# The batch loop of an attention and expert kernel is written out, and its down product changes sides

## The chip, the cores and the metric

The kernel runs on one core of one Trainium2 chip. The metric is the device time of one execution in microseconds (us), as the median of several runs. Five engines matter here: TensorE (PE in the rows, with its weight loads as PEld), VectorE (DVE), ScalarE (ACT), GpSimd (POOL) and SyncE (SP), which issues the transfers. Each works through its own list of instructions in order, and they wait for each other through semaphores.

## The reference

For a batch of 8 sequences of 1024 tokens with 256 channels, all in float32:

```python
# first half
qkv = x @ Wqkv + bqkv                       # q, k, v: 1024 x 256 each
q2, k2 = normalised squares of centred q, k
kv = einsum('bnc,bnd->bcd', k2, v)
t2 = einsum('bnc,bcd->bnd', q2, kv) / sqrt(N)
x1 = layernorm(x + (v + t2) @ Wln + bln)
# second half: 16 experts of width 128
sel    = sigmoid(einsum('bsd,ed->bse', x1, expert_sel))
scores = relu(einsum('bsd,edh->bseh', x1, keys))
out    = einsum('bseh,ehv,bse->bsv', scores, values, sel)
result = layernorm(x1 + out)
```

## The kernel before, in words

Every float32 operand of a product is split into a high part (`_h`) and a low part (`_l`), and `product` (line 990) makes three matmuls of it: high by high, high by low, low by high. Each matmul has its own weight load.

The second half sets the frame. A batch is 32 steps: two groups (`g`) of 512 tokens, 16 experts (`e`) each. In step `s` TensorE makes the up product of expert `e` into `up_bank[s % 2]`: hidden units by tokens, 6 matmuls of 512 columns. VectorE turns it into `gated` (relu times the spread gate `sel_all`, line 962), ScalarE copies the high part `gated_h` (line 509), VectorE subtracts to get `gated_l` (line 972). One step later (`LAG = 1`) TensorE adds the down product into two PSUM banks, `down_bank[0]` and `down_bank[1]`, which collect a group's 16 experts. GpSimd spreads the next gate row (line 495).

The first half of the next batch is laid between these products by a hand-written table, `LOOP["plan"]`: at each step it names the stages that TensorE runs between up and down product. QK projects queries and keys, GG adds to the k-by-x matrix, KS and KV finish it, QT transposes q, Y makes the layer's output, XT transposes `x1`, LG makes the gate logits. The stages in `RING_KINDS` share two PSUM banks, `ring_bank`, in turn; a stage waits until the stage two places before it has been read.

A group ends in step 16 (or in step 0 of the next batch). Before the change its down banks hold channels by tokens. ScalarE copies both to `oT` (the end of its `step`, lines 661 to 675; line 509 in the profile), the stage OT transposes them back with 4 transposes for each pair of token tiles (line 1108), and VectorE adds `x1` into `z` (line 923), followed by the statistics (lines 928, 931) and the scaling. The first down product of the next group waits for `o_copied`, since it overwrites the banks.

All engines run the same function `run`: the start (`it = -1`), batch 0, then a hardware loop over batches 1 to 6, then batch 7 and a short end (`it = 8`, table `LAST`). GpSimd has a loop of its own over the groups.

Of the kernel before, what the change touches and what calls it, by code (L numbers as in the profile page):

```python
# [26 lines left out]
ALU = mybir.AluOpType  # L27
# [60 lines left out]
RING_KINDS = ("QT", "Y", "XT", "LG", "OT", "KS", "KV")  # L88
# [30 lines left out]
def stages(it, s):  # L119

    out = []
    for kind, a in schedule(it)["plan"].get(s, ()):
        if kind == "OT":
# [18 lines left out]
def build_program(nc, x, xT, wqk, wvT, wln, b_qk, b_v, b_ln, esel, keys, values, ident_in, out):  # L142
    with ExitStack() as ctx:
# [6 lines left out]
        def sem(name):  # L150
# [48 lines left out]
        oT = sb("oT", [P, M, GN])  # L199
# [5 lines left out]
        w_stage = [oT[:].rearrange("p a n -> p (a n)"), z[:].rearrange("p a t c -> p (a t c)")]  # L205
# [55 lines left out]
        o_copied = sem("o_copied")  # L261
        (o_transposed, z_added, z_stated, z_aggregated, z_rooted, z_inverted, z_shift_made, out_made) = map(sem, (
            "o_transposed", "z_added", "z_stated", "z_aggregated", "z_rooted", "z_inverted",
# [29 lines left out]
        def ring_place(it, s, kind, a):  # L293

            rep = it if isinstance(it, int) else 1
            n = RING_AT[(rep, s, kind, a)]
            if n < 2:
                return ring_bank[n % 2], None, 0
            pit, ps, pkind, pa, poff = RING[n - 2]
            b = it + (pit - rep) + poff  # L300
            if pkind == "OT":
                return ring_bank[n % 2], z_added, out_pair(it + (pit - rep), poff, pa)
# [20 lines left out]
        def run(eng, step):  # L323

            for s in range(FIRST_STEP, STEPS):
                step(-1, s)
            for s in range(STEPS):
                step(0, s)
            with eng.Fori(1, B - 1) as it:
                for s in range(STEPS):  # L330
                    step(it, s)
            for s in range(STEPS):
                step(B - 1, s)
            for s in range(LAST_STEPS):
                step(B, s)
# [51 lines left out]
        def _(sp):  # L387
# [48 lines left out]
            def step(it, s):  # L436
                if isinstance(it, int) and (it, s) in PIECE_LOADS:
                    i = 2 + PIECE_LOADS.index((it, s))

                    sp.wait_ge(piece_lo, i - 1)  # L440
                    load_piece(i)
                if s == 0 and has(it, 1):
                    load_half(it, 0)
                if s == 7 and has(it, 1) and not (isinstance(it, int) and it < 0):
                    load_half(it, 1)
                for kind, a, off in planned(it, s, ("LG", "OT")):
# [11 lines left out]
        def _(pool):  # L458
# [43 lines left out]
            with pool.Fori(1, B * G) as grp:  # L502
                spread_group(grp)
# [3 lines left out]
        def _(act):  # L507
# [80 lines left out]
            def late(it, s):  # L588
                for kind, a, off in planned(it, s - 1, ("OT",)):
# [5 lines left out]
                for kind, a, off in transposed_first(  # L595
                        planned(it, s, ("QK", "GG", "KV", "QT", "Y", "XT", "LG", "OT"))):
# [39 lines left out]
                    elif kind == "OT":  # L636
                        n = out_pair(it, off, a)
                        act.wait_ge(z_aggregated, 2 * n)
                        nc.scalar.activation(z_std[:, a], z_mv[:, a, :, 1], ACT.Sqrt,
                                             bias=eps_ln[:]).then_inc(z_rooted, 1)  # L640

            def step(it, s):
# [18 lines left out]
                if (s - LAG) % E == E - 1 and step_exists(it, s, LAG):  # L661
                    f = step_no(it, s, LAG)
                    grp = 2 * it + ((s - LAG) // E)
                    if last_iteration(it):
                        act.wait_ge(last_half_made, 1)
                    else:
                        act.wait_ge(down_made, f + 1)

                    at_least(act, o_transposed, 2 * grp)
                    if first_group(it, (s - LAG) // E):  # L670

                        act.wait_ge(piece_lo, WPIECES)
# [11 lines left out]
        def _(dve):  # L684
# [108 lines left out]
            def early(it, s):  # L793
                for kind, a, off in transposed_first(
                        planned(it, s - 1, ("QK", "GG", "KS", "KV", "QT", "Y", "XT", "OT"))):
# [47 lines left out]
                    elif kind == "OT":  # L843
# [8 lines left out]
                        if last_iteration(it):  # L852
                            layer_norm(z[:, a, 1], z[:, a, 1], z_mv[:, a, 1],
                                       z_rstd[:, a, 1:2]).then_inc(last_out_made, 1)

            def late(it, s):
# [33 lines left out]
                for kind, a, off in planned(it, s, ("KS", "KV", "Y", "LG", "OT")):  # L890
# [23 lines left out]
                    elif kind == "OT":  # L914
                        n = out_pair(it, off, a)
                        t = GT * (off % G) + 2 * a
                        dve.wait_ge(o_transposed, n)

                        at_least(dve, stored[a], it * (16 * G) + off * 16)
                        if isinstance(it, int) and it == 0:  # L920

                            dve.wait_ge(piece_lo, WPIECES)
                        V.tensor_tensor(z[:, a].rearrange("p t c -> p (t c)"), ring_of(it, s, kind, a)[:],
                                        x1[:, t:t + 2].rearrange("p t c -> p (t c)"),
                                        ALU.add).then_inc(z_added, 1)
# [17 lines left out]
            def step(it, s):  # L943
# [21 lines left out]
                if last_iteration(it) and s == LAG - 1:  # L965
                    dve.wait_ge(down_made, B * STEPS)
                    at_least(dve, o_transposed, 2 * (G * B - 1))
                    V.tensor_copy(oT[:, 1], down_bank[1][:]).then_inc(o_copied, 1)
# [12 lines left out]
        def _(pe):  # L981
# [35 lines left out]
            def layer1(it, s):  # L1017
                for kind, a, off in planned(it, s, ("QK", "GG", "KS", "KV", "QT", "Y", "XT", "LG", "OT")):
# [82 lines left out]
                    elif kind == "OT":  # L1101
                        n = out_pair(it, off, a)
                        pe.wait_ge(o_copied, n - a - 1 + M)
                        for i in range(2):
                            for m in range(M):
                                j = (i * M + m) * P
                                t = 2 * a + i
                                last = nc.tensor.transpose(bk[:, j:j + P], oT[:, m, t * P:(t + 1) * P], ident[:])  # L1108
                        last.then_inc(o_transposed, 1)

            def step(it, s):
# [16 lines left out]
                if step_exists(it, s, LAG):  # L1128
# [61 lines left out]
```

## Time and profile before

| | before |
|---|---|
| median of 3 runs | 1080.75 us (1080.56 to 1083.31) |
| the profiled execution | 1078.57 us |
| its span, first to last instruction | 1076.7 us |
| PE busy | 1026.5 us, 95% |
| DVE busy | 802.1 us, 74% |
| ACT busy | 525.6 us, 49% |
| mean granted clock of TensorE | 0.987 of full speed |

The span is what the rows below divide up; the time of the execution has 1.87 us around it. Busy time of an engine is the union of its instructions, so TensorE, whose matmuls overlap each other in the pipeline, is read by the distance from one start to the next and not by the duration of one. A granted clock of 1.00 is 2.4 GHz, 0.50 is 1.2 GHz.

### The profile page before, as it was taken

What the parts mean: (1) busy time and instruction counts of PE and PEld (TensorE: products, weight loads), DVE (VectorE), ACT (ScalarE), POOL (GpSimd) and SP (SyncE); (2) the same over time, 40 slices, a digit from 0 to 9 for tenths busy, and PEclk for the clock granted to TensorE, in tenths of its full rate; (3) what the DMA queues carried; (4) which work ended last, traced back from release to release, by engine and by line L of the source; (5) the groups of instructions that cost most, each with busy time, mean ns of one, the idle gap of its engine ahead of it and who ended that gap; (6) DMA issues with size and microseconds to landing.
All of it is one profiled execution on the core that took longest, in us unless ns stands there. A gap on an engine that the chain in (4) does not pass through costs nothing.

```text
span 1076.7 us, 17466 instructions
## 1 busy us (share of the span) xinstructions
PE 1026.5 (95%) x5228; PEld 863.6 (80%) x5228; DVE 802.1 (74%) x1819; ACT 525.6 (49%) x1223; POOL 216.1 (20%) x273
## 2 busy tenths in 40 slices
PE   5789999999989999899998999989999899999996
PEld 4668888888868888688887888878888788888885
DVE  6888887878757877578775878668787678867564
ACT  5555643475334653356533565245653456434332
POOL 2121222212221121121122121221122112221221
PEclk9999999999999999899999999999999999999999
DMA  5031000100011000110001100011000110000000
GB/s 174 24 116 60 3 20 33 68 1 2 22 41 59 1 1 19 41 59 2 10 10 41 58 2 20 0 41 58 2 20 0 60 39 1 20 1 21 1 20 20
DMA packets 12089, 32.01 MB, mean 30 GB/s; under 512 B 1792, under 2 KB 2048, under 8 KB 12032
## 3 DMA queue, kind: packets, MB, share of 16 engines
q1 hardware_dynamic: 12032, 31.42, 8.4%
q14 instruction: 41, 0.34, 0.1%
q8 instruction: 16, 0.26, 0.1%
HBM read 22.50 MB, written 8.39 MB: 29 GB/s over the span
## 4 chain that ended last, share of the span: by engine, by line
PE 90%; DVE 4%; issue 3%; ACT 2%; DMA 0%; ACTq 0%; DVEq 0%
PE down_bank L990 32%; PE up_bank L990 32%; PE ring_bank L990 9%; PE qk_bank L990 8%; PE g_bank L990 4%; PE ring_bank L1108 1%; PE ring_bank L1089 1%; PE ring_bank L1073 1%; DVE gated L962 1%; PE ring_bank L1099 1%; PE ring_bank L1098 1%; PE ring_bank L1054 1%; ACT oT L509 0%; ACT gated_h L509 0%; DMA x<-in_wqk 0%
## 5 line engine op out<-in xcount | busy, mean ns | idle before, releaser
L509 ACT ACTIVATE gated_h<-gated 128x512 fp32r<-128x512 f32 x256 | 161.3, 630 | 397.3 <-DVE gated L962 397.3
L495 POOL PARTITION_BROADCAST sel_all<-sel_rows x240 | 193.0, 804 | 744.8 <-DVE gated L962 744.0
L962 DVE SCALAR_TENSOR_TENSOR gated<-up_bank,sel_all 128x512 f32<-128x512 f32 x256 | 176.0, 687 | 85.3 <-PE up_bank L990 69.3
L990 PE MATMUL down_bank<-gated_h,vals_h 128*128 128x512 f32 x512 | 210.2, 411 | 19.2 <-ACT oT L509 18.4
L972 DVE TENSOR_TENSOR gated_l<-gated,gated_h 128x512 fp32r<-128x512 f32 x256 | 179.0, 699 | 45.3 <-ACT gated_h L509 45.3
L990 PE MATMUL up_bank<-x1T_h,keys_h 128*128 128x512 f32 x512 | 202.8, 396 | 0.0
L990 PE MATMUL up_bank<-x1T_h,keys_l 128*128 128x512 f32 x512 | 202.6, 396 | 0.0
L990 PE MATMUL down_bank<-gated_h,vals_l 128*128 128x512 f32 x512 | 202.2, 395 | 0.0
L990 PE MATMUL down_bank<-gated_l,vals_h 128*128 128x512 f32 x512 | 201.6, 394 | 0.0
L990 PE MATMUL up_bank<-x1T_l,keys_h 128*128 128x512 f32 x512 | 200.7, 392 | 0.0
L990 PEld LDWEIGHTS down_bank<-gated_h,vals_h 128*128 128x128 f32 x512 | 96.9, 189 | 39.0 <-ACT oT L509 19.6
L990 PEld LDWEIGHTS up_bank<-x1T_h,keys_l 128*128 128x128 f32 x512 | 97.0, 189 | 22.2
L990 PEld LDWEIGHTS down_bank<-gated_h,vals_l 128*128 128x128 f32 x512 | 96.8, 189 | 22.4
L990 PEld LDWEIGHTS up_bank<-x1T_l,keys_h 128*128 128x128 f32 x512 | 97.1, 190 | 21.7
L990 PEld LDWEIGHTS up_bank<-x1T_h,keys_h 128*128 128x128 f32 x512 | 97.2, 190 | 20.3
L990 PEld LDWEIGHTS down_bank<-gated_l,vals_h 128*128 128x128 f32 x512 | 97.2, 190 | 15.2
L758 DVE TENSOR_TENSOR qk<-qk_bank,qk_bias 128x512 f32<-128x512 f32 x60 | 41.3, 688 | 36.2 <-PE qk_bank L990 36.2
L990 PE MATMUL qk_bank<-wqk_h,xT_h 128*128 128x512 f32 x120 | 49.7, 414 | 9.6 <-DVE xT_l L738 9.6
L990 PE MATMUL qk_bank<-wqk_h,xT_l 128*128 128x512 f32 x120 | 48.3, 402 | 0.0
L990 PE MATMUL qk_bank<-wqk_l,xT_h 128*128 128x512 f32 x120 | 48.2, 402 | 0.0
L771 DVE TENSOR_TENSOR y<-ring_bank,x_raw 128x256 f32<-128x256 f32 x64 | 27.0, 422 | 27.5 <-PE ring_bank L990 26.9
L509 ACT ACTIVATE k_h<-k,k_scale 128x256 fp32r<-128x256 f32 x64 | 32.6, 509 | 28.9 <-DVE k_scale L805 28.2
(160 smaller groups left out, 1710.2 us busy)
## 6 DMA issues: line engine op xcount, KB each, us to landing
xT_raw<-in_xT SPq DMA_DIRECT2D x16, 512.0 KB, 3.7
x_raw<-in_x SPq DMA_DIRECT2D x16, 512.0 KB, 4.6
out<-z SPq DMA_DIRECT2D x32, 256.0 KB, 2.5
oT<-in_keys SPq DMA_DIRECT2D x4, 512.0 KB, 4.2
z<-in_values SPq DMA_DIRECT2D x4, 512.0 KB, 4.4
sel_rows<-sel SPq DMA_DIRECT2D x64, 8.0 KB
x<-in_wqk SPq DMA_DIRECT2D x1, 512.0 KB, 3.4
sel_all<-in_b_qk SPq DMA_DIRECT2D x1, 256.0 KB, 6.1
```

The source lines that it names most:

```text
L495: nc.gpsimd.partition_broadcast(sel_all[:, e % 2], row, P).then_inc(sel_spread, 1)
L509: return nc.scalar.activation(dst, src, ACT.Copy, **kw)
L758: V.tensor_tensor(qk_of(it, t)[:], qk_bank_of(it, t)[:], qk_bias[:], ALU.add).then_inc(qk_biased, 1)
L771: V.tensor_tensor(y[:, a % 2], ring_of(it, s, "Y", a)[:, 0:C], x_raw[:, a], ALU.add).then_inc(y_added, 1)
L962: V.scalar_tensor_tensor(out=gated[:], in0=up_bank[s % 2][:], scalar=0.0, in1=sel_all[:, s % 2], op0=ALU.max, op1=ALU.mult).then_inc(gate_ ...
L972: V.tensor_tensor(gated_l[:, s % 2], gated[:], gated_h[:, s % 2].bitcast(F32), ALU.subtract).then_inc(gated_lo, 1)
L990: last = mm(dst, lhs, rhs, start=start and i == 0, stop=stop and i == n - 1, **kw)
L1054: last = mm(bk[:, j:j + 2], total[:, m * P:(m + 1) * P], ones[:, 0:2], start=True, stop=True)
L1073: last = nc.tensor.transpose(bk[:, j:j + P], q2[:, 2 * a + i, m * P:(m + 1) * P], ident[:])
L1089: last = nc.tensor.transpose(bk[:, m * P:(m + 1) * P], x1[:, a, m * P:(m + 1) * P], ident[:])
L1098: mm(bk[:], esel_hl[:, m], x1T_h[:, a, m], start=(m == 0), stop=False)
L1099: last = mm(bk[:], esel_h[:, m], x1T_l[:, a, m], start=False, stop=(m == M - 1))
```

## The change

Three things change. The hardware loops of all engines become Python loops, so that each engine's list of instructions holds all batches one after the other, with constants in its waits. The down product takes the gated tokens as weights and the values as the moving side, so that its banks hold tokens by channels: `down_bank[a]` has token tiles 2a and 2a+1, 256 columns each. And the stage OT goes: no copies to `oT`, no transposes; VectorE adds `x1` to a down bank directly (stage ZA, new function `add_zs`), and what followed the addition keeps its place as stage ZN. The staging buffer of the weights, which shared the room of `oT`, gets its own, `w_room`, of the same size.

```diff
 LOOP plan
-        0: [("QT", 2)], 1: [("QT", 3)], 2: [("OT", 0), ("Y", 4)], 3: [("OT", 1)], 4: [("Y", 5)],
+        0: [("QT", 2)], 1: [("ZA", 0), ("ZA", 1), ("QT", 3)], 2: [("ZN", 0), ("Y", 4)], 3: [("ZN", 1)], 4: [("Y", 5)],
...
-        16: [("GG", 5)], 17: [("QK", 7)], 18: [("GG", 6)], 19: [("KS", 0), ("OT", 0), ("GG", 7)],
-        20: [("OT", 1)], 21: [("KV", 0), ("QT", 0)], 22: [("QT", 1)], 23: [("Y", 0)],
+        16: [("GG", 5)], 17: [("ZA", 0), ("ZA", 1), ("QK", 7)], 18: [("GG", 6)], 19: [("KS", 0), ("ZN", 0), ("GG", 7)],
+        20: [("ZN", 1)], 21: [("KV", 0), ("QT", 0)], 22: [("QT", 1)], 23: [("Y", 0)],
...
-LAST = dict(plan={1: [("OT", 0), ("OT", 1)]}, split_xT={}, split_x={}, bias_x={}, scale_q={},
+LAST = dict(plan={1: [("ZA", 0), ("ZA", 1), ("ZN", 0), ("ZN", 1)]}, split_xT={}, split_x={}, bias_x={}, scale_q={},
...
 run
-            with eng.Fori(1, B - 1) as it:
+            for it in range(1, B):
                 for s in range(STEPS):
                     step(it, s)
-            for s in range(STEPS):
-                step(B - 1, s)
...
 gpsimd
-            with pool.Fori(1, B * G) as grp:
+            for grp in range(1, B * G):
                 spread_group(grp)
...
 scalar, at the end of step
-                    for m in range(M if not last_iteration(it) else 1):
-                        copy(oT[:, m], down_bank[m][:]).then_inc(o_copied, 1)
...
 vector
+            def add_zs(it, s):
+                for kind, a, off in planned(it, s, ("ZA",)):
+                    n = out_pair(it, off, a)
+                    t = GT * (off % G) + 2 * a
+                    if last_iteration(it) and a == 0:
+                        dve.wait_ge(last_half_made, 1)
+                    else:
+                        dve.wait_ge(down_made, it * STEPS + (off + 1) * E)
+
+                    at_least(dve, stored[a], it * (16 * G) + off * 16)
+                    if isinstance(it, int) and it == 0:
+
+                        dve.wait_ge(piece_lo, WPIECES)
+                    V.tensor_tensor(z[:, a].rearrange("p t c -> p (t c)"), down_bank[a][:],
+                                    x1[:, t:t + 2].rearrange("p t c -> p (t c)"),
+                                    ALU.add).then_inc(z_added, 1)
...
 vector, step
+                add_zs(it, s)
                 if step_exists(it, s):
                     f = step_no(it, s)
                     dve.wait_ge(up_made, f + 1)
...
 tensor, step
-                    if e == 0:
-
-                        at_least(pe, o_copied, M * grp)
-                    for c in range(M):
-                        r = (s - LAG) % 2
-                        if c == 1 and last_iteration(it):
+                    r = (s - LAG) % 2
+                    for t in range(GT):
+                        a, i = divmod(t, 2)
+                        if e == 0 and i == 0:
+
+                            at_least(pe, z_added, 2 * grp - 1 + a)
+                        if t == 2 and last_iteration(it):
                             last.then_inc(last_half_made, 1)
-                        last = product(down_bank[c][:], [(both(vals_h, vals_l, ALL, e, slice(c * P, (c + 1) * P)),
-                                                          both(gated_h, gated_l, ALL, r, ALL))],
-                                       start=(e == 0), stop=(e == E - 1))
+
+                        last = product(down_bank[a][:, i * C:(i + 1) * C],
+                                       [(both(gated_h, gated_l, ALL, r, slice(t * P, (t + 1) * P)),
+                                         both(vals_h, vals_l, ALL, e, ALL))],
+                                       start=(e == 0 and i == 0), stop=(e == E - 1),
+                                       skip_group_check=True)
                     last.then_inc(down_made, 1)
```

On TensorE, this is the first down product of a group before the change, in step 1 of the loop body, behind the transposes of QT 3:

```order
L1073 MATMUL ring_bank0<-ident,q2 128x128 x4
L1132 REGISTER_ALU
L285 REGISTER_ALU
L990 MATMUL down_bank0<-gated_h,vals_h 128x512
L990 MATMUL down_bank0<-gated_l,vals_h 128x512
L990 MATMUL down_bank0<-gated_h,vals_l 128x512
L990 MATMUL down_bank1<-gated_h,vals_h 128x512
L990 MATMUL down_bank1<-gated_l,vals_h 128x512
L990 MATMUL down_bank1<-gated_h,vals_l 128x512
```

And a down product now:

```order
L974 MATMUL down_bank0<-vals_h,gated_h 128x256
L974 MATMUL down_bank0<-vals_l,gated_h 128x256
L974 MATMUL down_bank0<-vals_h,gated_l 128x256
L974 MATMUL down_bank0<-vals_h,gated_h 128x256
L974 MATMUL down_bank0<-vals_l,gated_h 128x256
L974 MATMUL down_bank0<-vals_h,gated_l 128x256
L974 MATMUL down_bank1<-vals_h,gated_h 128x256
L974 MATMUL down_bank1<-vals_l,gated_h 128x256
L974 MATMUL down_bank1<-vals_h,gated_l 128x256
L974 MATMUL down_bank1<-vals_h,gated_h 128x256
L974 MATMUL down_bank1<-vals_l,gated_h 128x256
L974 MATMUL down_bank1<-vals_h,gated_l 128x256
```

Six matmuls of 512 columns have become twelve of 256, each with a weight load; the register instructions, which the loop's waits needed, are gone.

On VectorE, steps 0 to 2 of the loop body before (`gated` and `gated_l` are the two passes of each step, `z` is the addition of `x1`):

```order
L962 SCALAR_TENSOR_TENSOR gated<-up_bank0,sel_all 128x512
L972 TENSOR_TENSOR gated_l<-gated,gated_h 128x512
L831 ISA
L832 TENSOR_TENSOR qT_l<-ring_bank1,qT_h 128x512
L958 REGISTER_ALU
L962 SCALAR_TENSOR_TENSOR gated<-up_bank1,sel_all 128x512
L972 TENSOR_TENSOR gated_l<-gated,gated_h 128x512
L831 REGISTER_ALU
L832 TENSOR_TENSOR qT_l<-ring_bank0,qT_h 128x512
L958 REGISTER_ALU
L962 SCALAR_TENSOR_TENSOR gated<-up_bank0,sel_all 128x512
```

The addition of the first pair came behind this last row, in step 2, from `ring_bank1`. The same steps now, up to step 1:

```order
L950 SCALAR_TENSOR_TENSOR gated<-up_bank0,sel_all 128x512
L956 TENSOR_TENSOR gated_l<-gated,gated_h 128x512
L812 TENSOR_TENSOR qT_l<-ring_bank1,qT_h 128x512
L849 TENSOR_TENSOR z<-down_bank0,x1 128x512
L849 TENSOR_TENSOR z<-down_bank1,x1 128x512
L950 SCALAR_TENSOR_TENSOR gated<-up_bank1,sel_all 128x512
```

Both additions now stand one behind the other in step 1, ahead of that step's `gated`.

The end of VectorE's loop body before; the list of the changed kernel has no such branch on any engine but the one at its start and the one at its end:

```order
L962 SCALAR_TENSOR_TENSOR gated<-up_bank1,sel_all 128x512
L935 TENSOR_SCALAR q2<-q2,q_scale 128x256 x2
L972 TENSOR_TENSOR gated_l<-gated,gated_h 128x512
L329 REGISTER_ALU
L329 COMPARE_AND_BRANCH
```

The jump back, taken five times on each engine that runs `run`, is gone.

## Rows read from the trace of the kernel before

**Rows 1.** The page, busy time, share of the span, instructions.

```profile
PE 1026.5 (95%) x5228; PEld 863.6 (80%) x5228; DVE 802.1 (74%) x1819; ACT 525.6 (49%) x1223; POOL 216.1 (20%) x273
```

**Rows 2.** The waits: who waited for whom, total us, times, longest.

```profile
PE down_bank L990 <- ACT oT L509: 18.4, 5, 3.7
```

**Rows 3.** Windows: batch 1, then batches 2 to 6; PEclk is the granted clock.

```profile
189.00:314.80 125.80, 125.80 (x653) 106.57 (x652) 97.49 (x224) 63.64 (x150) 25.13 (x32) 1.00 0.07 25
314.80:969.30 654.50, 636.10 (x3261) 537.20 (x3260) 492.01 (x1127) 322.81 (x757) 129.30 (x161) 0.99 0.07 24
```

**Rows 4.** Timeline (start, duration, what, idle before) where batch 2 begins.

```profile
317.37 0.69 DVE L962 SCALAR_TENSOR_TENSOR gated<-up_bank,sel_all 128x512 f32<-128x512 f32 x1 [4.64 <-PE up_bank L990]
...
319.31 1.08 ACT L509 ACTIVATE oT<-down_bank 128x512 f32<-128x512 f32 x2
...
320.45 0.51 PE L990 MATMUL down_bank<-gated_h,vals_h 128*128 128x512 f32 x1 [3.64 <-ACT oT L509]
```

**Rows 5.** Windows: just behind that wait.

```profile
321.20:324.60 3.40, 3.40 (x9) 2.63 (x9) 1.49 (x2) 0.70 (x2) 0.73 (x1) 0.50 0.00 0
```

**Rows 6.** The chain that ended last, batch 2: start, us, what.

```profile
401.17 0.44 PE ring_bank L1108 x4
401.61 1.39 PE down_bank L990 x6
...
404.38 1.38 PE ring_bank L990 x12
...
412.17 1.42 PE ring_bank L990 x12
...
432.54 1.37 PE down_bank L990 x6
```

**Rows 7.** The same chain in batch 0: a GG stage, and KS.

```profile
97.49 0.70 PE g_bank L990 x6
...
139.31 0.79 PE ring_bank L1054 x8
```

**Rows 8.** Timeline of PE: first and last of 48 matmuls of stage Y.

```profile
46.84 0.36 PE L990 MATMUL ring_bank<-wvl_h,xT_h 128*128 128x256 f32 x1 [0.26 <-DVE kvw_l L827]
...
52.49 0.28 PE L990 MATMUL ring_bank<-kvw_h,qT_l 128*128 128x256 f32 x1
```

**Rows 9.** Groups of instructions by line: busy us, mean ns, idle before.

```profile
L1108 PE MATMUL ring_bank<-ident,oT 128*128 128x128 f32 x128 | 19.6, 277 | 0.9 <-DVE oT L968 0.9
```

**Rows 10.** Timeline of DVE and PE, steps 1 to 3 of batch 1.

```profile
189.52 0.68 DVE L832 TENSOR_TENSOR qT_l<-ring_bank,qT_h 128x512 fp32r<-128x512 f32 x1
190.61 0.69 DVE L962 SCALAR_TENSOR_TENSOR gated<-up_bank,sel_all 128x512 f32<-128x512 f32 x1 [0.41 <-PE up_bank L990]
190.76 0.48 PE L990 MATMUL down_bank<-gated_h,vals_h 128*128 128x512 f32 x1
...
197.46 0.66 DVE L972 TENSOR_TENSOR gated_l<-gated,gated_h 128x512 fp32r<-128x512 f32 x1
198.57 0.48 PE L990 MATMUL down_bank<-gated_h,vals_h 128*128 128x512 f32 x1
```

**Rows 11.** Timeline of DVE and PE, step 17 of batch 1.

```profile
256.86 0.68 DVE L744 TENSOR_TENSOR x_l<-x_raw,x_h 128x512 fp32r<-128x512 f32 x1
257.54 0.69 DVE L962 SCALAR_TENSOR_TENSOR gated<-up_bank,sel_all 128x512 f32<-128x512 f32 x1
258.75 0.39 PE L990 MATMUL down_bank<-gated_h,vals_h 128*128 128x512 f32 x1
```

**Rows 12.** Timeline of DVE at the end of the kernel.

```profile
1067.24 0.69 DVE L968 COPY oT<-down_bank 128x512 f32<-128x512 f32 x1 [1.74 <-PE down_bank L990]
...
1069.47 0.75 DVE L928 BATCH_NORM_STATS2 z_stats<-z 128x6 f32<-128x256 f32 x2
...
1070.36 0.67 DVE L923 TENSOR_TENSOR z<-ring_bank,x 128x512 f32<-128x512 f32 x1
...
1071.06 0.75 DVE L928 BATCH_NORM_STATS2 z_stats<-z 128x6 f32<-128x256 f32 x2
```

More of the change, by code:

```diff
@@ L83 @@
     gpsimd_xT=(1,), gpsimd_x=())
[L85 removed]
+LAST = dict(plan={1: [("ZA", 0), ("ZA", 1), ("ZN", 0), ("ZN", 1)]}, split_xT={}, split_x={}, bias_x={}, scale_q={},
             gpsimd_xT=(), gpsimd_x=())
 LAST_STEPS = 3
[L88 removed]
+RING_KINDS = ("QT", "Y", "XT", "LG", "KS", "KV")
 FIRST_STEP = min(FIRST["split_xT"])
@@ L122, in stages @@
     for kind, a in schedule(it)["plan"].get(s, ()):
-        if kind == "OT":
+        if kind in ("ZA", "ZN"):
             g = 0 if s >= E else -1
@@ L198, in build_program @@
         gated_h, gated_l = sb("gated_h", [P, 2, GN], F32R), sb("gated_l", [P, 2, GN], F32R)
-        oT = sb("oT", [P, M, GN])
+        w_room = sb("w_room", [P, WPIECE])
         z = sb("z", [P, 2, 2, C])
@@ L202, in build_program @@
         z_std, z_rstd, z_shift = (sb(n, [P, 2, 2]) for n in ("z_std", "z_rstd", "z_shift"))
-        w_stage = [oT[:].rearrange("p a n -> p (a n)"), z[:].rearrange("p a t c -> p (a t c)")]
+        w_stage = [w_room[:], z[:].rearrange("p a t c -> p (a t c)")]
         wqk_raw = x1[:, 0:4, :].rearrange("p (m a) c -> p m a c", m=M)
@@ L260, in build_program @@
         last_half_made = sem("last_half_made")
-        o_copied = sem("o_copied")
-        (o_transposed, z_added, z_stated, z_aggregated, z_rooted, z_inverted, z_shift_made, out_made) = map(sem, (
-            "o_transposed", "z_added", "z_stated", "z_aggregated", "z_rooted", "z_inverted",
+        (z_added, z_stated, z_aggregated, z_rooted, z_inverted, z_shift_made, out_made) = map(sem, (
+            "z_added", "z_stated", "z_aggregated", "z_rooted", "z_inverted",
             "z_shift_made", "out_made"))
@@ L445, in step @@
                     load_half(it, 1)
-                for kind, a, off in planned(it, s, ("LG", "OT")):
+                for kind, a, off in planned(it, s, ("LG", "ZN")):
                     if kind == "LG":
@@ L588, in late @@
             def late(it, s):
-                for kind, a, off in planned(it, s - 1, ("OT",)):
+                for kind, a, off in planned(it, s - 1, ("ZN",)):
                     n = out_pair(it, off, a)
@@ L595, in late @@
                 for kind, a, off in transposed_first(
-                        planned(it, s, ("QK", "GG", "KV", "QT", "Y", "XT", "LG", "OT"))):
+                        planned(it, s, ("QK", "GG", "KV", "QT", "Y", "XT", "LG", "ZN"))):
                     b = it + off
@@ L635, in late @@
                         copy(sel[:], ring_of(it, s, kind, a)[LOW:LOW + E, :]).then_inc(logits_low, 1)
-                    elif kind == "OT":
+                    elif kind == "ZN":
                         n = out_pair(it, off, a)
@@ L660, in step @@
                     weights_hi(PIECE_STEPS.index((it, s)))
[L661 to L672, printed above, removed]
-                    for m in range(M if not last_iteration(it) else 1):
-                        copy(oT[:, m], down_bank[m][:]).then_inc(o_copied, 1)
             act.wait_ge(constants_set, 4)
@@ L794, in early @@
                 for kind, a, off in transposed_first(
-                        planned(it, s - 1, ("QK", "GG", "KS", "KV", "QT", "Y", "XT", "OT"))):
+                        planned(it, s - 1, ("QK", "GG", "KS", "KV", "QT", "Y", "XT", "ZN"))):
                     b = it + off
@@ L842, in early @@
                                         ALU.subtract).then_inc(x1T_lo, 1)
-                    elif kind == "OT":
+                    elif kind == "ZN":
                         n = out_pair(it, off, a)
@@ L889, in late @@
                         V.reciprocal(q_scale[:], q_root[:]).then_inc(q_scale_set, 1)
-                for kind, a, off in planned(it, s, ("KS", "KV", "Y", "LG", "OT")):
+                for kind, a, off in planned(it, s, ("KS", "KV", "Y", "LG", "ZN")):
                     b = it + off
@@ L913, in late @@
                                         ALU.add).then_inc(logits_summed, 1)
-                    elif kind == "OT":
+                    elif kind == "ZN":
                         n = out_pair(it, off, a)
[L916 to L925, printed above, removed]
                         dve.wait_ge(z_added, n)
@@ L964, in step @@
                                            op1=ALU.mult).then_inc(gate_applied, 1)
[L965 to L968, printed above, removed]
                 late(it, s)
@@ L1017, in layer1 @@
             def layer1(it, s):
-                for kind, a, off in planned(it, s, ("QK", "GG", "KS", "KV", "QT", "Y", "XT", "LG", "OT")):
+                for kind, a, off in planned(it, s, ("QK", "GG", "KS", "KV", "QT", "Y", "XT", "LG")):
                     b = it + off
@@ L1100, in layer1 @@
                         last.then_inc(logits_made, 1)
[L1101 to L1109, printed above, removed]
             def step(it, s):
```

2 lines of the change are left out of this document (removed).

## Prediction

> **What bounds the kernel now.** I read the page first, for the engine that is busiest: TensorE is busy 95% of the span, VectorE 74% [rows 1]. So the question is what TensorE executes and where it stands still. The chain that ended last answers the first: from batch 0 on it is TensorE's stages one behind the other with no gap, an up or down product of six 512-column matmuls at 1.37 to 1.39 us, a Y stage of twelve 256-column matmuls at 1.42, a pair's OT transposes at 0.44 [rows 6]. A microsecond taken off TensorE's list there is a microsecond of the span. The waits answer the second: behind the start-up, TensorE's one large idle time is 18.4 us in 5 waits of up to 3.7 us for ScalarE's copy `oT` [rows 2].
>
> Windows by batch then say where these five are. Batch 1, the first pass of the loop, lasts 125.8 us with TensorE busy all through. Batches 2 to 6 last 654.5 us, 130.9 each, with the same 652 to 653 matmuls per batch [rows 3]. Each pass behind a jump back costs 5.1 us more than the pass without one; in all 654.5 - 5 x 125.8 = 25.5 us. The timeline at the start of batch 2 shows how. VectorE stood idle 4.64 us before its first `gated` of the new pass; ScalarE's `oT` copy, behind it, came at 319.31; TensorE's first down product of the next group, which overwrites the copied banks, waited 3.64 us for that [rows 4]. Right behind the wait the granted clock is 0.50, that is 1.2 in place of 2.4 GHz, for 3.4 us [rows 5], in which TensorE does half the work: 1.7 us more. The 25.5 us are the 18.4 of waits and about 7 of clock.
>
> **The change part by part.**
>
> *The loops written out, -25.4 us.* The delay sits at the jump back and nowhere else: batch 1 is loop code too, run for the first time, and has none [rows 3, 4]. Without jumps batches 2 to 6 should last as long as batch 1. I take 25.4. The Trainium skill, Runtime: NRT & Kernel Launch, section Instruction fetch mechanics, says that a taken branch whose target lies outside the fetched pages forces a fetch before execution goes on. The trace agrees: 4.64 us of idle VectorE at the jump.
>
> *OT's transposes go, -13.2 us.* There are 128 of them in 32 pairs [rows 9]. Two pairs lie in the tail, counted below. The other 30 stood in the chain at 0.44 us each [rows 6]: 30 x 0.44 = 13.2. ScalarE's `oT` copies lay beside TensorE's work except at the loop's waits; ScalarE is half idle [rows 1], so they bring nothing further.
>
> *The down product, +8.5 us.* Columns stay the same (6 x 512 = 12 x 256), but weight loads double, 1536 more in 256 steps. The price is that of twelve 256-column matmuls with a load each, and the trace has three such cases: KV 1.38 us for twelve, Y 1.42 [rows 6], and GG 0.70 for six, so 1.40 [rows 7]. The hardest is the start of batch 0, where 48 come in a row: from 46.84 to 52.49 is 5.65 / 47 = 0.120 us each, 1.44 for twelve [rows 8]. A down product now takes 1.375: most stand at 1.37, those behind transposes at 1.39 [rows 6]. Per step this is +0.005 (KV) to +0.065 (48 in a row), times 256: +1 to +17 us. The new product has GG's form, few matmuls of three to each half bank, and stands beside a busy VectorE like Y: 1.408 between these two, +0.033 x 256 = 8.5. What hides a weight load is the stream of the matmul before it. The load alone can be bounded by KS, eight matmuls of 2 columns in 0.79 us, 0.099 each [rows 7]; a 256-column matmul, at 0.115 to 0.120, still covers it, but with only some 0.02 us to spare.
>
> The Trainium skill has a rule that speaks against this part: TensorE: Matmul & The Clock Gate, section LDWEIGHTS, gives a load of 128 columns 128 / 1.2 = 107 ns, as an estimate, just as long as 256 columns at 2.4 GHz take. Unhidden, that would be 1536 x 0.107 = +164 us and a time of about 1204; the rows of Y and KV say that it is hidden.
>
> *The additions move ahead of `gated`, +2.4 us.* In step 1 VectorE now runs `qT_l` (189.52 to 190.20), both additions (0.68 each, as at the tail [rows 12]), and only then `gated`, at 191.6 in place of 190.61 [rows 10]. The first down product of the group wants bank 0 at 190.76; the addition ends at 190.88, so TensorE waits some 0.2 us with the semaphore. Bank 1 is wanted six matmuls later, 0.7 us, when the second addition just ends. Behind the late `gated` wait ScalarE's `gated_h`, VectorE's `gated_l`, GpSimd's next gate row, and two products later TensorE; `gated_l` would be ready some 2.1 us behind the start of `gated`, at 193.7; before its product TensorE still has the down product of 190.96, an up product and a Y, 4.2 us, so it is wanted at about 195.2. In step 3 the margin is thin: `gated_l` ended at 198.12 and its product began at 198.57 after OT [rows 10]; without OT's 0.44 it is wanted at 198.1. I give 0.35 us to each of the 7 batches behind the first for both places. At step 17 QK's 1.4 us gives room: `x_l` ends at 257.54, the additions at 258.2 and 258.9, the product comes at 258.75 and reaches bank 1 at 259.4 [rows 11]: nothing. The same two additions leave steps 2, 3, 19 and 20, so VectorE's load stays. If the cover were gone everywhere, 15 x 1.37 = 21 us at most; below nothing it cannot go.
>
> *The tail, -2.2 us.* Before, VectorE's copy of bank 1 stood at 1067.24, then transposes, then an addition, and the statistics began at 1069.47 and 1071.06 [rows 12]. Now the addition of bank 1 takes the copy's place and ends at 1067.93, bank 0 having been added during the last product. The first statistics begin there, the second 0.89 later (1070.36 - 1069.47) at 1068.82: 2.24 us earlier than 1071.06, and all behind them with them.
>
> *At nothing:* the separate staging room (same size), the shorter ring (Y 4 now waits for QT 2, an earlier reader), register instructions gone from TensorE's sequencer, which had matmuls ahead of it in any case.
>
> Sum: -25.4 - 13.2 + 8.5 + 2.4 - 2.2 = -29.9 us. Against the profiled execution's 1078.57 this gives 1048.7. The median of the runs shown is 2.2 us above that execution; runs with one or two more half-clock stretches at the jumps would explain it, and these go as well. I say 1049, 2.9% under the median.
>
> **The rivals.**
>
> *Weight loads come out from behind the stream; slower.* The new weights are the gated tokens, written just before, and the list never relaxes to 512-column matmuls for long. If half of each load (0.05 us) showed on the 1536 added ones, +76 us in place of +8.5: 1116. All other terms give -38.4, so it decides at 0.15 us per step, that is when a 256-column matmul takes 0.127 us. Against it: no row goes beyond 0.120, not even 48 in a row.
>
> *The stall was not the jump.* If straight lists of this length make the engines wait for their instructions as the jump did, the 25.4 us stay: 1074, still 0.6% under the median; somewhat more such waits make it no change. Against it: batch 0 is straight code in the kernel before, and its rows stand one behind the other as batch 2's do; batch 1 was fetched for the first time too and shows TensorE busy for all of its 125.8 us [rows 3].
>
> *VectorE becomes late at every group's end.* ZA in front of `gated` costs its 1.37 us in 15 places, 21 us in place of 2.4: 1067. For it speaks the thin margin in step 3, against it step 17's room and that TensorE never waited for `gated_l` inside a batch.
>
> *The 0.120 of the 48 holds:* +17 in place of +8.5, 1057; part of the forecast's range.
>
> **How the numbers follow.** Forecast with the down term between +1 and +17 and the boundary between 0 and 5: 1039 to 1060, chance 0.80. VectorE late 0.08 (1060 to 1070). Waits for instructions 0.06, two thirds of it still faster. Weight loads 0.05 (slower). Better than 1039: 0.01. The range 1039 to 1061 leaves out a little under 2 in 10. A measurement here tells about 0.3% from no change; faster 0.92, same 0.03, slower 0.05.
>
> **What the changed profile would show.** TensorE's chain without L1108; no wait for ScalarE's copy; batches 1 to 6 alike at 125.8 - 4 x 0.44 + 32 x 0.033 + 0.3 = 125.4 us; granted clock 1.00 from batch 0 to 7; a down product of twelve at 1.38 to 1.44 us; a wait of down for VectorE's `z` of about 0.2 us in step 1 and none in step 17; the last statistics about 2 us closer to the last matmul. The prediction is wrong if twelve take over 1.5 us, if batches still differ by 5 us, or if TensorE waits for `z` or `gated_l` more than 1 us a batch.

## The result and the profile after

| | before | after |
|---|---|---|
| median of 4 runs | 1081.94 us | 1045.52 us (1041.46 to 1046.57) |
| ratio to before | | 0.966, 95% interval 0.963 to 0.969 |
| the profiled execution | 1078.57 us | 1041.46 us |
| its span | 1076.7 us | 1039.6 us |
| TensorE's mean granted clock | 0.987 | 0.995 |

The kernel is 36 us faster; 1049 was forecast. The busy times of the page after, beside [rows 1]:

```profile
PE 1008.7 (97%) x6636; PEld 914.7 (88%) x6636; DVE 796.1 (77%) x1818; ACT 509.2 (49%) x1192; POOL 219.9 (21%) x273
```

TensorE executes 1408 matmuls more (1536 added, 128 transposes gone) and is busy 18 us less, in a span 37 us shorter. The windows answer to [rows 3]; a batch is again taken from step 1 to step 1:

```profile
187.50:312.30 124.80, 124.80 (x831) 113.74 (x829) 97.63 (x226) 62.33 (x148) 26.32 (x32) 1.00 0.08 27
312.30:935.90 623.60, 623.60 (x4143) 568.50 (x4142) 488.06 (x1126) 311.49 (x736) 131.58 (x160) 1.00 0.07 25
```

Batches 2 to 6 last 124.7 us each, no longer 130.9, TensorE is busy for all of it, and the granted clock is 1.00. The surplus of the passes behind a jump is gone, and a batch is 1.0 us below batch 1 of before as well. Three of the waits of TensorE:

```profile
PE qk_bank L974 <- DVE xT_l L718: 9.8, 1, 9.8
...
PE g_bank L974 <- DVE k_l L870: 6.3, 4, 2.6
...
PE down_bank L974 <- DVE gated_l L956: 0.8, 1, 0.8
```

The view has seven more rows, of 0.2 to 1.7 us; all but the last of the three shown lie before batch 1, and that one is the very last product. Nothing takes the place of the 18.4 us of [rows 2]. The chain, beside [rows 6]:

```profile
404.28 1.36 PE down_bank L974 x12
...
407.01 1.42 PE ring_bank L974 x12
408.43 0.22 PE ring_bank L1073 x2
408.65 1.42 PE down_bank L974 x12
410.06 1.40 PE up_bank L974 x6
...
417.27 1.36 PE down_bank L974 x12
418.63 1.37 PE up_bank L974 x6
```

A down product of twelve takes 1.36 to 1.42 us here, at its cheapest less than six long ones did (in the whole chain of batches 1 to 6 single ones go up to 1.51); an up product behind it is at times 1.40 instead of 1.37.

### The profile page after: what moved, and what is told of

The parts are those of the page before. It is cut to its first block, busy times and chain, and to the rows that moved or that the text cites. A ratio compares the mean times of both kernels' runs of the same rounds, so it can differ in the third digit from the quotient of the medians.

```text
span 1039.6 us, 18353 instructions
## 1 busy us (share of the span) xinstructions
PE 1008.7 (97%) x6636; PEld 914.7 (88%) x6636; DVE 796.1 (77%) x1818; ACT 509.2 (49%) x1192; POOL 219.9 (21%) x273
## 2 busy tenths in 40 slices
DMA packets 12122, 32.59 MB, mean 31 GB/s; under 512 B 1792, under 2 KB 2048, under 8 KB 12032
## 4 chain that ended last, share of the span: by engine, by line
PE 95%; DVE 3%; ACT 1%; issue 0%; DMA 0%; ACTq 0%
PE down_bank L974 34%; PE up_bank L974 34%; PE ring_bank L974 10%; PE qk_bank L974 8%; PE g_bank L974 4%; PE ring_bank L1073 1%; PE ring_bank L1057 1%; PE ring_bank L1083 1%; PE ring_bank L1082 1%; PE ring_bank L1038 1%; DMA x<-in_wqk 0%; DVE keys_l L927 0%; DVE k_l L870 0%; DVE qk L738 0%; DVE q L922 0%
## 5 line engine op out<-in xcount | busy, mean ns | idle before, releaser
L490 POOL PARTITION_BROADCAST sel_all<-sel_rows x240 | 196.8, 820 | 710.6 <-DVE gated L950 709.9
L974 PE MATMUL down_bank<-vals_h,gated_h 128*128 128x256 f32 x1024 | 292.0, 285 | 0.9 <-DVE gated_l L956 0.8
L974 PE MATMUL down_bank<-vals_l,gated_h 128*128 128x256 f32 x1024 | 285.3, 279 | 0.0
L974 PE MATMUL down_bank<-vals_h,gated_l 128*128 128x256 f32 x1024 | 285.3, 279 | 0.0
L956 DVE TENSOR_TENSOR gated_l<-gated,gated_h 128x512 fp32r<-128x512 f32 x256 | 173.3, 677 | 43.5 <-ACT gated_h L504 42.5
L974 PEld LDWEIGHTS down_bank<-vals_h,gated_h 128*128 128x128 f32 x1024 | 193.2, 189 | 9.1 <-DVE gated_l L956 3.2
L974 PEld LDWEIGHTS down_bank<-vals_l,gated_h 128*128 128x128 f32 x1024 | 192.9, 188 | 4.6
L974 PEld LDWEIGHTS down_bank<-vals_h,gated_l 128*128 128x128 f32 x1024 | 192.7, 188 | 0.0
L974 PEld LDWEIGHTS up_bank<-x1T_h,keys_h 128*128 128x128 f32 x512 | 96.7, 189 | 11.1
```

Of the source, the lines that this page charges most:

```text
L490: nc.gpsimd.partition_broadcast(sel_all[:, e % 2], row, P).then_inc(sel_spread, 1)
L956: V.tensor_tensor(gated_l[:, s % 2], gated[:], gated_h[:, s % 2].bitcast(F32), ALU.subtract).then_inc(gated_lo, 1)
L974: last = mm(dst, lhs, rhs, start=start and i == 0, stop=stop and i == n - 1, **kw)
```

## The experiments

Times are medians on the device; "before" was run beside each. Where two variants are compared, I use windows over batches 2 to 6, since the start differs from execution to execution by some us (last section).

**Loops written out, nothing else.**

```diff
 kernel before
-            with eng.Fori(1, B - 1) as it:
+            for it in range(1, B):
                 for s in range(STEPS):
                     step(it, s)
-            for s in range(STEPS):
-                step(B - 1, s)
...
-            with pool.Fori(1, B * G) as grp:
+            for grp in range(1, B * G):
```

> The kernel before with the hardware loops written out on every engine and nothing else changed. Theory (the jump back costs a fetch, then a wait, then a half clock): all of batches 1 to 6 last about 125.8 us, the five waits of TensorE for the oT copy are gone, and the time falls by about 25 us, to some 1055. Rival (the list of instructions has to be fetched anyway, and the gain of the changed kernel is that of the product): under 5 us gained.

Measured: 1056.82 us, ratio 0.977 (0.974 to 0.980), 23.5 us less than the 1080.27 of before. Windows over batch 1 and over batches 2 to 6:

```profile
190.00:315.80 125.80, 125.80 (x653) 106.59 (x653) 97.53 (x226) 64.53 (x152) 26.55 (x33) 1.00 0.08 27
315.80:944.90 629.10, 629.10 (x3261) 532.92 (x3261) 487.76 (x1126) 322.74 (x756) 132.84 (x161) 1.00 0.08 26
```

All batches last 125.8 us, as batch 1 of before did: 654.5 - 629.1 = 25.4 us are the loops. The rival falls.

**The new product and ZA, with the hardware loops of before.**

```diff
 changed kernel
-            for it in range(1, B):
+            with eng.Fori(1, B - 1) as it:
                 for s in range(STEPS):
                     step(it, s)
+            for s in range(STEPS):
+                step(B - 1, s)
...
-            for grp in range(1, B * G):
+            with pool.Fori(1, B * G) as grp:
```

> The changed kernel with the hardware loops of before put back on every engine. Theory (the parts add up): transposes -13, tail -2, twelve shorter matmuls +3 to +8 us, so about 8 to 12 us less than before, near 1071; the five waits at the jumps stay at 3.5 to 4.5 us each, now for VectorE's addition in place of ScalarE's copy. Rival (the written-out list helped only since it went with the new product, or the other way round): the sum of this gain and that of the kernel with the loops written out alone misses 37 us by more than 5.

Measured: 1063.77 us, ratio 0.986 (0.982 to 0.989), 16.5 us less than before by medians. With the 23.5 of the variant above the parts make 40, and the two profiled executions differ by 37: 3 apart, within the rival's 5. But my figure of 1071 was 7 too high, and the waits were not the ones that I expected. The view of them:

```profile
PE up_bank L976 <- issue: 12.1, 5, 2.7
```

TensorE's five idle times now stand before its own first up product of a pass, end by nothing that another engine does ("issue"), and are 2.25 to 2.75 us long, not 3.6 to 3.7. The stall had changed its engine, which I had not expected. So each engine was given a loop of its own.

**A loop on one engine at a time.** The edit to the changed kernel, here for VectorE (`nc.scalar` and `nc.tensor` in the others):

```diff
+        LOOPED = (nc.vector,)
...
-            for it in range(1, B):
+            if eng in LOOPED:
+                with eng.Fori(1, B - 1) as it:
+                    for s in range(STEPS):
+                        step(it, s)
                 for s in range(STEPS):
-                    step(it, s)
+                    step(B - 1, s)
+            else:
+                for it in range(1, B):
+                    for s in range(STEPS):
+                        step(it, s)
```

> The changed kernel with the hardware loop put back on VectorE alone. Theory: VectorE is idle for 3.5 to 5 us at each jump, TensorE then waits about 2 to 3 us for gated_l at the group's start; 10 to 20 us above the changed kernel. Rival (ScalarE's jump was the late one): no difference.

Measured: 1069.45 us, ratio 0.988 (0.984 to 0.992), 24 us above the changed kernel, more than the 10 to 20 expected. VectorE's timeline at the first jump back, and TensorE's waits:

```profile
314.65 0.67 DVE L965 TENSOR_TENSOR gated_l<-gated,gated_h 128x512 fp32r<-128x512 f32 x1
319.01 0.69 DVE L959 SCALAR_TENSOR_TENSOR gated<-up_bank,sel_all 128x512 f32<-128x512 f32 x1 [3.69 <-PE up_bank L983]
```

```profile
PE down_bank L983 <- DVE z L858: 16.3, 5, 3.7
```

VectorE stands idle 3.69 us; the releaser named, the up product, had long been done (TensorE had gone on to the next one at 317.39), so the wait is the engine's own. TensorE pays 16.3 us of it, for `z` and not for `gated_l` as I had expected. Much of the rest of the 24 is clock: the stretch behind the first wait, 322.45 to 326.00, has a granted clock of 0.52. This is the stall of [rows 4]: VectorE late at the same place of the pass, and TensorE waiting for what comes behind it.

> The changed kernel with the hardware loop of before put back on TensorE alone. Theory (each engine pays for its own jump when its loop body is long; TensorE's body has grown by 192 matmuls a batch with the new product): TensorE stands still about 2.5 us at each of the five jumps, with no other engine late, as in the kernel with all loops and the new product; 12 to 20 us above the changed kernel. Rival (TensorE's jump is free and the wait comes from the engines that feed it): batches alike at 124.8 us.

Measured: 1064.80 us, ratio 0.984 (0.976 to 0.991), 19 us above the changed kernel.

```profile
PE up_bank L983 <- issue: 12.9, 5, 2.8
```

> The changed kernel with the hardware loop put back on ScalarE alone. Theory: ScalarE needs as long for its jump as VectorE, but stands idle about half the time, and is late with gated_h by some 2 us; TensorE waits 0 to 2 us per jump; 0 to 12 us above the changed kernel. Rival (only VectorE's jump costs): no difference.

Measured: 1046.50 us, ratio 0.967 (0.964 to 0.969), the time of the changed kernel; batches 2 to 6:

```profile
314.50:938.30 623.80, 623.80 (x4142) 568.27 (x4141) 488.05 (x1126) 311.51 (x736) 131.61 (x161) 1.00 0.08 27
```

ScalarE's jump costs nothing here (its idle time at the jump, 2.22 us, is that of the changed kernel, 2.21); the rival of that run holds, and the middle of my 0 to 12 us was too high. In the kernel before TensorE's longest wait was named after ScalarE's copy, but what was late was VectorE, from which ScalarE gets `gated`. With loops on all engines the waits of 16 us and 13 us do not add. From the first stalled pass to the fifth, a pass takes 128.1 us in the kernel with all loops and the new product (313.20 to 825.41), 129.7 with VectorE's loop alone (322.45 to 841.06) and 124.7 with none. That both engines then stand still at once is my reading; the runs show only that the stalls overlap. GpSimd's loop was not tried alone.

**Why TensorE's jump was free before.** Its loop alone, once on the kernel with the old product and once with the old product cut as below:

> The kernel before, old product and OT, loops written out on all engines but TensorE. Theory (the cost of a jump depends on the length of the body it jumps over: TensorE's old body, 653 matmuls and their loads, showed no gap at the jump before): batches 1 to 6 alike at 125.8 us, same as with all loops written out. Rival (TensorE's gap was there but hidden behind the wait for VectorE and ScalarE): a gap of 2 us or more at each jump.

Measured: 1055.55 us, ratio 0.975 (0.972 to 0.977), as with no loop at all. Batches 2 to 6:

```profile
314.00:943.00 629.00, 629.00 (x3262) 532.82 (x3261) 487.62 (x1126) 322.60 (x756) 132.79 (x161) 1.00 0.08 26
```

> The kernel before with old orientation, OT and the down product cut into 256-column halves, loops written out on all engines but TensorE: a loop body as long as the changed kernel's and longer (653 + 192 matmuls) with the old product. Theory (the jump costs when the body is too long): a gap of about 2.5 us for TensorE at each of five jumps, 12 to 20 us above the same kernel without the loop. Rival (the new product, not the length, brought TensorE's gap): no gap, batches alike at 126.8 us.

Measured: 1079.52 us, ratio 0.998 (0.996 to 1.000), 17 us above the same kernel without the loop (1062.85); by windows a pass takes 129.6 us in place of 126.8, 14 us in five.

```profile
PE up_bank L997 <- issue: 12.9, 5, 3.0
```

Same product, 192 matmuls and loads more in the body, and the gap is there. So it is the length of the body that TensorE jumps back over, 653 matmuls with their loads or 845, and not the new product. With waits and register instructions the traces have 1399 instructions of TensorE between two jumps in the first case, 1783 in the second, and 1744 with the new product.

The pages of the profile also count the packets that fetch instructions (packets, MB, share). Kernel with TensorE's loop and the short body, kernel with TensorE's loop and the new product:

```profile
q14 instruction: 37, 0.30, 0.1%
q8 instruction: 16, 0.26, 0.1%
```

```profile
q8 instruction: 65, 1.06, 0.4%
q14 instruction: 37, 0.30, 0.1%
```

The short body is that of the old product. The packets of all variants:

| packets | no loop | TensorE's | VectorE's | ScalarE's | all |
|---|---|---|---|---|---|
| q8, short body | 42 | 16 | not run | not run | 16 |
| q14, short body | 37 | 37 | not run | not run | 41 |
| q8, new product | 53 | 65 | 53 | 53 | 65 |
| q14, new product | 37 | 37 | 51 | 29 | 41 |

Queue q8 follows TensorE's list alone. With the short body it brings nothing at all between 300 and 960 us of the kernel before: TensorE goes round on what it holds. With a long one it brings more packets than the straight list takes (also with the old product in halves, 65 against 54), and in the kernel with the new product and TensorE's loop the first gap, 310.20 to 313.00, has one that starts at 310.29. VectorE's loop, with 384 instructions between two jumps, adds 14 packets, so its body too is fetched anew; ScalarE's, with 284, saves 8: this body is held, and ScalarE's jump is free.

The Trainium skill, Runtime: NRT & Kernel Launch, section Instruction fetch mechanics, has instructions fetched in blocks into a store that is larger for TensorE (2048 instructions) than for most others (512), with a stall when a branch leaves what is held. The trace agrees with the store and the stall; but TensorE's body is fetched anew at 1744 instructions and VectorE's at 384, so a body shorter than the page's figure can still be fetched anew. Where between 1399 and 1744, and between 284 and 384, the limit lies no run here shows.

**Twice the loads with the old product.**

```diff
 kernel before, loops written out
-                        last = product(down_bank[c][:], [(both(vals_h, vals_l, ALL, e, slice(c * P, (c + 1) * P)),
-                                                          both(gated_h, gated_l, ALL, r, ALL))],
-                                       start=(e == 0), stop=(e == E - 1))
+                        for w in range(2):
+                            cols = slice(w * C, (w + 1) * C)
+                            last = product(down_bank[c][:, cols],
+                                           [(both(vals_h, vals_l, ALL, e, slice(c * P, (c + 1) * P)),
+                                             both(gated_h, gated_l, ALL, r, cols))],
+                                           start=(e == 0 and w == 0), stop=(e == E - 1),
+                                           skip_group_check=True)
```

> The kernel before with loops written out, and each 512-column matmul of the down product cut into two of 256 columns with the same weights, so 1536 more weight loads as in the changed kernel, but values still as weights and OT still there. Theory (a 256-column matmul hides its own load at 0.114 to 0.120 us): twelve take 1.37 to 1.44 us, 2 to 8 us more than the same kernel without the cut. Rival (the cheap pitch comes from the gated tokens being the weights): twelve take over 1.45 us, 20 us or more on top.

Measured: 1062.85 us, ratio 0.983 (0.980 to 0.987), 6.0 us above the uncut kernel. Batches 2 to 6 last 634.0 in place of 629.1:

```profile
317.70:951.70 634.00, 634.00 (x4223) 577.55 (x4222) 488.51 (x1126) 322.96 (x756) 133.07 (x161) 1.00 0.08 26
```

That is 0.98 us a batch, 0.031 a step, 7.8 us in 256 steps for 1536 loads. So 1536 more matmuls with their loads cost little with the old weights too; with the new ones it was at most 5.3 us (see the section on the prediction).

**Still more short matmuls.** The up product of the changed kernel is cut into halves in the same way.

> The changed kernel with the up product cut into 256-column matmuls too, another 1536 weight loads, so that batch 0 to 7 has hardly any 512-column matmul but QK's and LG's. Theory (each 256-column matmul covers the next load by itself): up takes 1.37 to 1.44 us in place of 1.38, 0 to 15 us more than the changed kernel. Rival (the long matmuls between give TensorE's sequencer or its loads time to run ahead): the pitch of 256 columns goes beyond 0.125 us and the time rises by 30 us or more.

Measured: 1049.29 us, ratio 0.972 (0.969 to 0.975). Batches 2 to 6 last 625.2 in place of 623.6:

```profile
314.50:939.70 625.20, 625.20 (x5103) 612.77 (x5102) 488.52 (x1126) 311.49 (x736) 131.53 (x160) 1.00 0.08 25
```

0.32 us a batch, 2.6 us in all for another 1536 loads. With hardly a long matmul left, TensorE is still busy for the whole stretch; weight loads are busy 98% of these windows (612.77 of 625.20).

**Shorter than a load.** The moving side of the down product is cut to 128 columns, all else as in the changed kernel.

```diff
-                        last = product(down_bank[a][:, i * C:(i + 1) * C],
-                                       [(both(gated_h, gated_l, ALL, r, slice(t * P, (t + 1) * P)),
-                                         both(vals_h, vals_l, ALL, e, ALL))],
...
+                        for w in range(2):
+                            last = product(down_bank[a][:, i * C + w * P:i * C + (w + 1) * P],
+                                           [(both(gated_h, gated_l, ALL, r, slice(t * P, (t + 1) * P)),
+                                             both(vals_h, vals_l, ALL, e, slice(w * P, (w + 1) * P)))],
```

> The changed kernel with each 256-column matmul of the down product cut into two of 128 columns with the same weights: 24 matmuls and 24 loads a step. Theory (a load alone takes about 0.10 us and is hidden only behind a longer stream): the pitch is that of the load, 0.099 to 0.11 us, a down product takes 2.4 to 2.65 us in place of 1.38, and the kernel 250 to 320 us more. Rival (loads are hidden at any length): 24 x 0.06 = 1.5 us, 20 to 40 us more.

Measured: one run, 1372.01 us. The chain:

```profile
403.81 2.63 PE down_bank L974 x24
406.44 1.44 PE up_bank L974 x6
```

24 matmuls take 2.63 us, 0.110 each, nearly twice the 0.057 that would be half of a 256-column matmul's pitch, and close to the 0.099 that a matmul of 2 columns took with its load [rows 7]. So the pair of load and matmul has a least pitch that the columns do not set. I take it for the load's; a fixed price of the pair would show the same, and no run here has narrower weights to tell them apart. A 256-column matmul, at 1.36 to 1.42 us for twelve, has a pitch of 0.113 to 0.118. The cover is complete and has next to no room, 0.003 to 0.008 us. Cost: about 327 us over the changed kernel, just over the top of the expectation.

**The additions behind `gated`.**

```diff
 changed kernel, VectorE's step
-                add_zs(it, s)
                 if step_exists(it, s):
...
                                            op1=ALU.mult).then_inc(gate_applied, 1)
+                add_zs(it, s)
                 late(it, s)
```

> The changed kernel with both additions moved behind the step's gated on VectorE, so that TensorE's first product of a group gets its banks one VectorE pass later. In the changed kernel's profile the additions end 0.1 us before TensorE wants bank 1 and TensorE waits well under 0.1 us. Theory (the place ahead of gated is just early enough): in step 1 TensorE now waits for z, 0.6 to 1.4 us in each of 7 batches, in step 17 0 to 0.6 us; 5 to 13 us above the changed kernel. Rival (the banks are never the limit): no difference.

Measured: 1056.61 us, ratio 0.976 (0.973 to 0.978), 11 us above the changed kernel.

```profile
PE down_bank L974 <- DVE z L849: 8.7, 8, 1.5
```

Seven waits of 1.03 or 1.04 us in step 1, as expected, and one of 1.47 in step 17 of batch 7; step 17 is free in the other batches. The waits are 8.7 of the 11 us that the place ahead of `gated` is worth.

## Why the prediction was right, point by point

**Loops, -25.4 us: right in size, whose jump it was left open.** 25.4 measured by windows. The prediction read VectorE idle first and ScalarE's copy behind it, but did not ask which engine's jump costs what. Loops on single engines, tried with the new product, show that VectorE's jump made the stall, ScalarE's none, and that TensorE's would have made one had its body been as long as it is now. Putting the new product under the old loops would have moved the stall to TensorE. The clock's part, 25.4 - 18.4 = 7.0 us, is not five times the 1.7 us of the first wait: the granted clock was 0.50 for some 3.4, 6.8 and 3.4 us at the first three waits and stayed at 1.00 at the other two.

**OT's transposes, -13.2 us, and the down product, +8.5.** Between the kernel with loops written out and the changed one, batches 2 to 6 differ by 629.1 - 623.6 = 5.5 us, 1.10 a batch. Four pairs of transposes are 1.76 of it by [rows 6], so product and boundary together cost 0.66 a batch, 0.021 a step, 5.3 us in 256 steps. The term was 8.5 alone: too high. I had put twelve matmuls at 1.408, between GG and Y; 1.375 + 0.021 is 1.396, between KV and GG. The cause of Y's slower pitch was not tried.

**The additions ahead of `gated`, +2.4 us: too high, by a term that I had in hand.** Step 1 of batch 2 in the profile after, beside [rows 10]:

```profile
312.66 0.69 DVE L812 TENSOR_TENSOR qT_l<-ring_bank,qT_h 128x512 fp32r<-128x512 f32 x1
313.27 1.28 DVE L849 TENSOR_TENSOR z<-down_bank,x 128x512 f32<-128x512 f32 x2
314.46 0.68 DVE L950 SCALAR_TENSOR_TENSOR gated<-up_bank,sel_all 128x512 f32<-128x512 f32 x1
```

```profile
313.69 0.60 PE L1057 MATMUL ring_bank<-ident,q 128*128 128x128 f32 x4
314.10 0.36 PE L974 MATMUL down_bank<-vals_h,gated_h 128*128 128x256 f32 x1
```

The first product starts 0.41 us after the transposes; one step earlier, where nothing waits, it is 0.35 (310.45 to 310.80). So it waits some 0.06 us, not 0.2: the two additions run back to back in 1.28 us, less than twice 0.68. In step 3 I let `gated_l` end at the old time, though its engine had an addition less in step 2:

```profile
319.64 0.66 DVE L956 TENSOR_TENSOR gated_l<-gated,gated_h 128x512 fp32r<-128x512 f32 x1
```

```profile
321.07 0.28 PE L974 MATMUL down_bank<-vals_h,gated_h 128*128 128x256 f32 x1
```

It ends at 320.30 and is wanted at 321.07. There is 0.77 us of room where I saw none. Both places together cost about 0.4 us in the kernel, an estimate from 0.06 in 7 batches.

**The tail, -2.2 us.** Measured from the start of the last down product, whose first matmul stood at 1031.08:

```profile
1032.09 1.37 DVE L849 TENSOR_TENSOR z<-down_bank,x 128x512 f32<-128x512 f32 x2 [1.06 <-PE down_bank L974]
1033.38 0.74 DVE L915 BATCH_NORM_STATS2 z_stats<-z 128x6 f32<-128x256 f32 x2
...
1034.26 0.72 DVE L915 BATCH_NORM_STATS2 z_stats<-z 128x6 f32<-128x256 f32 x2
```

The second statistics begin 3.18 us after it and the span ends 8.5 after it; before, with that product's first matmul at 1065.56, it was 5.50 us [rows 12] and 11.1. Gain 2.3 to 2.6.

**The sum.** -25.4 - 13.2 + 5.3 - 2.6 = -35.9 us, against -37.1 between the two profiled executions. The remaining 1.2 us are of the start: the mean granted clock over the first 75 us was 0.95 in this execution and 0.93 in the one before, 0.02 x 75 = 1.5 us of full-clock work, and batch 1 begins at 187.5 in place of 189.0. I take that for the spread of the last section, which is argued and not shown. A batch was forecast at 125.4 us and took 124.7, the two terms above. The forecast of -29.9 thus missed by 7.2 us: 5.6 in product and boundary, 0.4 in the tail, 1.2 in the start.

That 1049 lies only 3.5 us from the median is partly luck. I subtracted from the profiled execution, which lies 2.2 us below the median then known and 3.4 below that of all four runs, and argued that the spread would go with the jumps. It did not: the four executions after lie 5.1 us apart, those before 2.8.

**The rivals.** Loads did not come out from behind the stream, not even with 1536 more of them; with 128 columns the least pitch of load and matmul shows at once, for 327 us. The straight lists show no wait of the kind that the jump made, though the changed kernel fetches 53 packets of instructions for TensorE in place of 16. VectorE is not late at a group's end, and one pass later it would be.

## What to carry to other kernels

A wait that recurs once per pass of a hardware loop and ends in "issue", or in an engine that had long been done, may be the jump back. Compare the packets of the instruction queues with those of the straight list, and try the loop on each engine alone: here it cost 24 us on VectorE, 19 on TensorE and nothing on ScalarE, and it depended on the length of the body, so a change that only lengthens one engine's body can create it.

Turning a product round so that its result comes out in the wanted layout saves the copies and the transposes. It was nearly free with 256 columns streamed to each load of 128 (5.3 us at most for 1536 more pairs) and cost 327 us with 128 columns; nothing between was measured. When a stage moves, take its old work off the times at the old place too, not only add it at the new one.

## What the runs showed of the hardware that I had not expected

The spread between executions of one kernel, 1041.5 to 1046.6 us for the changed one, seems to lie in the start. Windows over the first 75 us of the changed kernel, of the one with loops written out, and of that one with halves:

```profile
0.00:75.00 75.00, 51.87 (x287) 43.12 (x288) 57.28 (x134) 43.73 (x112) 14.88 (x23) 0.95 0.32 105
```

```profile
0.00:75.00 75.00, 51.61 (x243) 42.49 (x244) 53.31 (x126) 39.06 (x107) 13.29 (x21) 0.89 0.32 99
```

```profile
0.00:75.00 75.00, 52.91 (x253) 44.53 (x254) 53.83 (x126) 39.14 (x107) 13.43 (x22) 0.84 0.30 99
```

TensorE waits for other engines several times there, and its granted clock averages 0.95, 0.89 and 0.84. From 0.95 to 0.84 is 16 us more at 1.2 GHz in place of 2.4. In batches 2 to 6 all gapless variants ran at 1.00. For the four executions of the changed kernel there is the mean granted clock of the whole: 0.995 in the one of 1041.46 us, 0.989 to 0.991 in those of 1045.5 to 1046.6, so the longer ones ran longer at the lower clock. I did not profile several executions of one kernel, so that it happens in the start is argued and not shown.
